# VectorE instead of GpSimd multiplies each head's attention output by its reciprocal sums

## The reference

```python
ada = silu(c) @ W_ada + b_ada                      # shift, scale and gate, twice
h   = layernorm(x) * (1 + scale_msa) + shift_msa
q, k, v = split(h @ W_qkv + b_qkv)                 # 16 heads of 36
o   = softmax((q * 36**-0.5) @ k.T) @ v            # per head
x   = x + gate_msa * (o @ W_proj + b_proj)
h   = layernorm(x) * (1 + scale_mlp) + shift_mlp
x   = x + gate_mlp * (gelu(h @ W_fc1 + b_fc1) @ W_fc2 + b_fc2)
# second layer
U, _ = qr(P)                                       # P is (576, 64)
R = expm(A(silu(c) @ W.T + b))                     # A is antisymmetric, 64 x 64
z = x @ U
x = x + (z @ R - z) @ U.T
```

## Time and profile before

| what | us |
|---|---|
| median of three runs | 2994.21 |
| range of the runs | 2987.70 to 2996.78 |
| the profiled execution, device time | 2989.66 |
| its span from first to last instruction | 2987.6 |
| TensorE busy | 2653.3 (89%) |
| VectorE busy | 1456.9 (49%) |
| ScalarE busy | 1081.5 (36%) |
| GpSimd busy | 920.5 (31%) |

### The profile page before, as it was taken

One profiled execution on the slowest core, in us unless ns is written; L12 is line 12 of the kernel. 1 busy time (PEld: TensorE's weight loads), 2 busy tenths in 40 slices (PEclk: granted clock), 3 DMA queues, 4 the chain that ended last, 5 costly groups with the idle time before them and its releaser, 6 DMA issues. The chain is left out here.

```text
span 2987.6 us, 49987 instructions
## 1 busy us (share of the span) xinstructions
PE 2653.3 (89%) x15289; PEld 2107.4 (71%) x15289; DVE 1456.9 (49%) x2960; ACT 1081.5 (36%) x2297; POOL 920.5 (31%) x1978
## 2 busy tenths in 40 slices
PE   5789979899797897989967488999999999999998
PEld 1556656567565665656644277999999999999997
DVE  3577676766767666666651452222222222222221
ACT  1265555555554554545550212222222222222221
POOL 1154444535444454454551730110111111111110
PEclk9799999989898998999986658999999999999998
DMA  6122121221212212122112511010101010110100
GB/s 203 35 65 63 49 82 43 70 60 57 75 45 64 60 56 72 45 65 63 56 44 86 168 50 41 25 35 25 35 25 35 25 35 29 30 33 27 33 23 24
DMA packets 90996, 160.95 MB, mean 54 GB/s; under 512 B 23488, under 2 KB 34960, under 8 KB 90704
## 3 DMA queue, kind: packets, MB, share of 16 engines
q1 hardware_dynamic: 77840, 110.61, 12.8%
q0 software_dynamic: 11856, 46.60, 4.7%
q10 hardware_dynamic: 1024, 0.26, 0.0%
HBM read 80.23 MB, written 20.30 MB: 34 GB/s over the span
## 5 line engine op out<-in xcount | busy, mean ns | idle before, releaser
L1598 PE MATMUL bank<-h2T,w 128*128 128x256 f32 x4032 | 583.9, 290 | 7.4 <-issue 4.6
L1598 PEld LDWEIGHTS bank<-h2T,w 128*128 128x128 f32 x4032 | 525.2, 190 | 47.5 <-issue 6.0
L1511 DVE TENSOR_TENSOR glo<-bank,ghi 128x256 fp32r<-128x256 f32 x288 | 122.2, 424 | 814.4 <-ACT bank L1488 814.3
L1611 PE MATMUL bank<-w,ghi 128*128 128x288 f32 x2304 | 494.8, 307 | 0.0
L1487 ACT ACTIVATE ghi<-bank,b 128x256 fp32r<-128x256 f32 x288 | 136.7, 475 | 835.8 <-PE bank L1598 835.8
L706 ACT ACTIVATE phi<-bank 128x512 fp32r<-128x512 f32 x512 | 303.0, 592 | 304.5 <-PE bank L999 276.8
L834 DVE TENSOR_TENSOR plo<-pf,phi 128x512 fp32r<-128x512 f32 x512 | 366.0, 715 | 90.8 <-ACT pf L709 85.8
L827 DVE TENSOR_REDUCE negm<-bank 128x1 f32<-128x512 f32 x512 | 349.6, 683 | 114.0 <-PE bank L971 97.5
L1611 PEld LDWEIGHTS bank<-w,ghi 128*128 128x128 f32 x2304 | 362.7, 188 | 37.8 <-issue 11.5
L1611 PE MATMUL bank<-w,glo 128*128 128x288 f32 x1152 | 339.1, 294 | 0.0
L709 ACT ACTIVATE pf<-bank 128x512 f32<-128x512 f32 x512 | 302.6, 591 | 0.0
(11 more groups left out here) (208 smaller groups left out, 3506.1 us busy)
## 6 DMA issues: line engine op xcount, KB each, us to landing
xln<-x POOLq DMA_DIRECT2D x16, 1152.0 KB, 6.5
qs<-qkhi SPq DMA_DIRECT2D x192, 72.0 KB
ks<-qkhi SPq DMA_DIRECT2D x192, 72.0 KB
wst<-w_fc POOLq DMA_DIRECT2D x34, 288.0 KB, 3.1
x_d<-xln POOLq DMA_DIRECT2D x32, 288.0 KB, 2.5
xa<-x_d SPq DMA_DIRECT2D x32, 288.0 KB, 2.8
xs<-x_d SPq DMA_DIRECT2D x16, 576.0 KB, 3.9
out<-xs SPq DMA_DIRECT2D x16, 576.0 KB, 2.9
```

Of the source, the lines that this page charges most:

```text
L1598: mm = pe.matmul(F[ft % 2][:, 0:CH], w1[0:rows, w, ft * PAR:(ft + 1) * PAR], h[0:rows, a, :], start=(i == 0), stop=(i == len(PASSES) - 1))
L1611: mm = pe.matmul(Y[2 * tt + half][:, 0:HALF], g[ft % 2][:, span], w2[:, ft, w, half * HALF:(half + 1) * HALF], start=(ft == 0 and i == 0), ...
```

## The change

`divide` goes from GpSimd's queue to the end of `read_o` on VectorE. The product now follows the sum directly, behind a wait for that sum's own semaphore, and it takes along the two waits for the destination buffers (`early_moved` for head 0, the last output transpose for head 5). The wait for `o_norm` in `read_o` goes. The start value of `o_norm` is set on VectorE. In `load_next_x` one wait is added, for the second x alone, since that load is no longer ordered behind a `divide`.

```diff
@@ gpsimd @@
-                pool.sem_inc(o_norm, 2)
...
                 def load_next_x(b):
                     if not isinstance(b, int) or b >= 2:
                         pool.wait_ge(x1_out, 16 * TT * (b - 1))
+                    if isinstance(b, int) and b == 1:
+                        pool.wait_ge(g_full, g_use(-1, ("ln", KT)) + 1)
                     load_x(pool, b)
...
-                def divide(b, n):
-
-                    h = (n // TT - 1) % HEADS
-                    pool.wait_ge(o_read, b * HEADS + n // TT + 1)
...
-                    pool.tensor_tensor(head, oraw[h % 2][:, :, :], recip[h % 2][:, :].unsqueeze(2).to_broadcast([PAR, TT, HD]), ALU.mult).then_inc(o_norm, 1)
...
                 def slot(b, n, phase):
-                    if n % TT == 3 and is_there(b, n - TT):
-                        divide(b, n)
@@ vector @@
+                dve.sem_inc(o_norm, 2)
...
                     dve.wait_ge(oT, ho + 3)
-                    dve.wait_ge(o_norm, ho + 1)
                     dve.reciprocal(recip[i][:, :], view[:, :, HD]).then_inc(recip_done, 1)
...
                     dve.tensor_reduce(oraw[i][:, :, :], pair, AX.X, ALU.add).then_inc(o_read, 1)
+                    h = (n // TT - 1) % HEADS
+                    if h < EARLY:
+                        if h == 0 and (not isinstance(b, int) or b >= 1):
+                            dve.wait_ge(early_moved, b)
+                        head = early[:, :, h * HD:(h + 1) * HD]
+                    else:
+                        if h == EARLY and (not isinstance(b, int) or b >= 1):
+                            dve.wait_ge(g_full, g_use(b, ("tr", TT - 1)) + 1)
+                        head = oo[:, :, h * HD:(h + 1) * HD]
+                    dve.wait_ge(o_read, ho + 2)
+                    dve.tensor_tensor(head, oraw[i][:, :, :], recip[i][:, :].unsqueeze(2).to_broadcast([PAR, TT, HD]), ALU.mult).then_inc(o_norm, 1)
```

## The result

| | before | after |
|---|---|---|
| median of 20 runs each, us | 2992.08 | 3001.68 |
| range, us | 2984.42 to 3005.19 | 2993.82 to 3012.22 |
| ratio to before (95%) | 1 | 1.0036 [1.0026, 1.0045] |
| span of the profiled execution, us | 2987.6 | 3000.0 |

The change makes the kernel slower by 0.36%, which is 10.8 us, with an interval of 7.8 to 13.5 (the two medians alone lie 9.6 us apart). The forecast was 3001 us, with a sum of 6.8 us.

What follows compares the result with a forecast made beforehand. TensorE was taken to bound the attention stage. Terms 2.4 + 0.8 + 1.8 + 1.4 + 0.4 = 6.8 us on 2994.2 gave 3001 us; own range 2996 to 3006, full range 2990 to 3015.

Steps and rivals of the forecast that it cites:

- What bounds, and what was removed: Attention stage: TensorE sets the pace; the 128 GpSimd products of 426 ns are not waited for inside the rounds.
- The product and d: VectorE, head ends: new product takes 0.30 us; d, the shift of everything behind it, is 0.34 us.
- The rival with 0.50: Larger shift of 0.50 us on VectorE exceeds many hiding gaps: 13.3 us, 3007 us; chance 0.22.
- Slot 46: VectorE runs from sum to `plo` without a gap; the whole 0.34 us passes in 7 rounds: 2.4 us.
- Slot 42: Chain to the low part of x: 0.14 us in three sign rounds, 0.34 in round 0, none in Cholesky: 0.8 us.
- Slots 30 to 33: Residual's addition starts 0.30 us later behind the gated projection; TensorE waits that much more for mask 8, six rounds: 1.8 us.
- Round 0 and the end: Round 0, slots 10, 18, 22, 34: 1.4 us; last rounds, 0.27 and 0.33 us less 0.17 at the transpose: 0.4 us.
- The unchanged waits: Slots 40 and 49: broadcast waits stay; GpSimd's busy time falls by 54.5 us, VectorE's rises by 38.
- The rival of the lock: VectorE and GpSimd exclude each other; elimination step runs beside slots 41 and 42: 2.4 to 5 us more, 3005 us; chance 0.15.
- The faster rival: GpSimd gets out of the way of VectorE's `plo` subtractions: some 8 us come back, 2993 us; chance 0.13.

Runs made afterwards that it cites:

- no product: Changed kernel without any product: VectorE's sum goes straight to the head's place, the output lacks the division; ratio 0.9997 to the kernel before.
- the reordered kernel that has the product in this very place: Changed kernel with GpSimd's elimination step ahead of the inversion (slot 39) and row mask ahead of the residual load (slot 48); ratio 0.9928 to the kernel before.
- product on both: Kernel before with GpSimd's product kept and the same product again on VectorE, into a tile nobody reads; ratio 1.0108 to the kernel before.
- one slot later: Changed kernel with every product moved to the next slot on VectorE, behind its `plo` and ahead of its units; ratio 1.0009 to the kernel before.
- heads 3 and 6 late: Changed kernel with only the products of slots 18 and 30 moved to slots 19 and 31, behind `plo`; ratio 1.0025 to the kernel before.
- four heads late: Changed kernel with products moved from slots 18 and 30 to 19 and 31, and from 42 and 46 to the end of 49; ratio 1.0031 to before.
- before, reordered: Kernel before, product on GpSimd, with the elimination step ahead of slot 39's inversion and the mask ahead of slot 48's residual load; 2955.56 us, ratio 0.9877.

## Why the prediction was right, and where its sum was not

- **What bounds, and what was removed.** Right. Without any product the time is 0.9997 of before, so GpSimd's products were hidden and nothing is won by their going.
- **The product and d.** Right in size: 0.308 us for 0.30, and d = 0.34. The rival with 0.50 falls. The Trainium skill, "VectorE: DVE Perf Modes", section "The TRN2 errata", gives (N+151)/0.96 ns for an fp32 addition of two tensors with N elements. The trace agrees for this product too: by the formula it would be an estimated 307 ns at 144 elements, with 308 measured, and 195 ns at 36, with 196 to 199 measured.
- **Slot 46.** The step "the whole 0.34 us passes, in 7 rounds" was too large: the wait at slot 47 is 0.54 us in nearly every round, not 0.9. Before, it had been 0.54 in two of seven rounds and 0 to 0.34 in the others, so the row chosen for the earlier trace rows was the largest of its kind. 1.8 us for 2.4.
- **Slot 42.** 2.9 us for 0.8 (it shows as the wait of slot 43). This wait varies between 1.25 and about 2.3 us a round within one trace. Its sum is 10.1 in the trace with no product and 9.6 in the reordered kernel that has the product in this very place, so about 2 us of the 2.9 may be chance.
- **Slots 30 to 33.** Right in size for the three sign rounds, 2.55 to 2.89 us for +0.30, though part of it is again the lock: the mask at the end stands 0.03 us behind the new product and takes 0.59 us, where it took 0.44. Wrong for the three Cholesky rounds, where the step "it waits 0.30 us more" came to 1.14. The step left out the lock on GpSimd's side. I had asked where a `plo` would have to give way to GpSimd, and not where a GpSimd instruction had just been ahead of a `plo` and would no longer be. Round 7 was not in the sum at all: its wait in slot 33 goes from 0.90 to 1.73 us.
- **Slot 21.** Not among the forecast's terms: the gap in slot 18 does take up VectorE's shift, as forecast, but the mask behind it was 0.11 us ahead of `plo` and is now behind it. 2.5 us for 0.
- **Round 0 and the end.** Right for round 0, 0.63 to 0.96 us at the first place and 1.3 us for 1.4 in all, and for the last transpose, which waits 0.17 us less. The 0.27 and 0.33 us of the last rounds don't show: in round 7 slot 43 had a wait of 0.23 us and has none now, and the broadcast of slot 57 is waited for 2.59 us before and after.
- **The unchanged waits.** Right for slots 40 and 49 together, +0.4 on 71.9 us. Busy times went by +32.0 us on VectorE and -45.5 on GpSimd, for +38 and -54.5: GpSimd's other instructions grew by 9 us. Some 4 of them are the 64x192 mask, which went from a mean of 844 to 911 ns by the lock.
- **The rival of the lock** had the mechanism and not the place: it looked at the step of slots 41 and 42, and it was slots 21, 32 and 33. Its reason against, that GpSimd is idle when the sum ends, is true and beside the point, since what counts is who is first some microseconds later. The rule that the forecast took from the Trainium skill ("SBUF — State Buffer", section "Who interferes with whom") is what these rows show, in both directions, and a start 0.04 us ahead decides it.
- **The faster rival** falls: `plo` went from 715 to 712 ns, 1.4 us in all.

The direction of the forecast, slightly slower, held because the mechanism of the shift was right; the largest single piece of the loss, the order of starts at slots 32, 33 and 21, was not in it. The sum, 6.8 us, lies just outside the measured 7.8 to 13.5; slots 33 and 21 are 6.2 us of what was missing (5.5 + 2.5 - 1.8), and with them it would have been 13.0. That the forecast of 3001 us lies within 1 us of the measured median is luck: it started from a median of three runs, 2994.2 us, where the 20 runs gave 2992.1, and this made up for part of a sum that was too small. Of the chances, 0.48 had gone to no difference and 0.42 to slower by over 0.3%; the measured 0.36% lies in the second, with an interval that reaches across the line.

The forecast also took a wait in the trace for time, one for one, and traces seem to break this: the kernel with no product has 5.6 us more waits than before and the same span. The missing term is TensorE's own busy time. From the first `plo` to the last every kernel runs the same 5849 TensorE instructions, and the stage is its waits and its busy time, with 0.5 to 1.4 us over (in us, one trace each):

| kernel | waits | TensorE busy | stage | granted clock |
|---|---|---|---|---|
| before | 177.9 | 1255.4 | 1434.1 | 0.93 |
| changed | 191.2 | 1257.7 | 1449.8 | 0.93 |
| no product | 183.5 | 1253.0 | 1437.1 | 0.93 |
| product on both | 202.2 | 1278.0 | 1481.6 | 0.91 |
| one slot later | 186.8 | 1251.3 | 1438.9 | 0.94 |
| heads 3 and 6 late | 187.0 | 1250.9 | 1438.8 | 0.93 |
| four heads late | 187.8 | 1259.9 | 1448.4 | 0.93 |
| before, reordered | 150.6 | 1249.6 | 1400.7 | 0.94 |

The same work takes TensorE longer at a lower granted clock. Executions of one kernel differ by it too: of the 29 of the kernel before beside the first experiments, the fastest took 2984.24 us at a mean clock of 0.928 and the slowest 2999.55 at 0.921, an estimated 2 us for 0.001. So of the 15.7 us between the two traces of the change 13.3 are waits, and the ratios of the experiments, which lie up to 7 us apart, hold some us of clock besides the waits that were meant to be tested. The waits in the named slots are what those experiments show. Whether a kernel's order also sets the clock that it is granted, or these executions happened to get it, no run here tells.

## What to carry to other kernels

Where two engines lock each other out, a shift of a few tenths of a microsecond can turn round who is first, and what was held becomes the holder: list all pairs that start within the shift of each other, in both directions, and look which of the two the bounding engine waits for. Read a wait in all rounds before you multiply one of its rows. Beside the waits, add up the busy time of the engine that bounds: where its clock can change, the same waits can go with another time. And look first at the largest wait in the profile. Here it was 92 us for an elimination that stood, in two slots, behind work it did not need. The order of the queue took 29 us of it and gave 1.23%, and all the moving of the product gave at best nothing.

## What the runs showed of the hardware that I had not expected

- The margin decides. With GpSimd 0.08 us ahead it keeps 0.59 us and VectorE's 0.68 becomes 1.06; with VectorE 0.04 us ahead GpSimd's 0.59 becomes 1.10.
- A short product that starts behind a long addition of the other engine is held for nearly all of it: 0.31 us became 1.50.
- The price hardly depends on who is held. It is what is left of the holder's time, less 0.13 or 0.14 us: 1.12 us of 1.25 for `plo` in the earlier trace rows, 0.17 of 0.30 for `plo` and 0.51 of 0.65 for the update in slot 32, 0.51 of 0.64 for the mask behind it, 1.19 of 1.33 for the product. One pair of these rows is cheaper: at slot 21 before, `plo` starts when the mask has 0.66 us left, and pays 0.17.
- The program with both products waits up to 3.01 us for VectorE at the start of a loop round, beside the 2.5 to 3.4 us that every kernel loses there.
- The same product costs GpSimd 426 ns and VectorE 308.
